# Second layer of a decoder kernel: GpSimd adds the exponentials of all six key tiles before TensorE sums them

## What is computed

```python
q = (Q @ Wq + bq).reshape(B, L, H, E)
k = (K @ Wk + bk).reshape(B, S, H, E)
v = (V @ Wv + bv).reshape(B, S, H, E)
scores = jnp.einsum('blhe,bshe->bhls', q, k)
A = jax.nn.softmax(scale * scores, axis=-1)
out = jnp.einsum('bhls,bshd->blhd', A, v).reshape(B, L, H * E)
return out @ We + be
```

## Time and profile before

| | |
|---|---|
| runs | 4483.24, 4483.69, 4485.51 us |
| the profiled execution | 4486.9 us |
| its span in the trace | 4485.1 us |
| mean granted TensorE clock | 0.864 |
| layer 2 in the trace | about 1380 to 2995 us |
| TensorE busy | 3463.7 us (77%) |
| VectorE, ScalarE, GpSimd busy | 57%, 38%, 14% |

### The profile page before, as it was taken

How to read it: one execution, slowest core, us unless ns; L and a number is a source line. 1 busy time by engine, 2 the same in 40 slices (tenths; PEclk the granted TensorE clock), 3 DMA queues, 4 the chain that set the end, 5 groups by cost and what they waited for, 6 DMA issues and landing times. The chain is left out here.

```text
span 4485.1 us, 77233 instructions
## 1 busy us (share of the span) xinstructions
PE 3463.7 (77%) x31129; PEld 2505.9 (56%) x31170; DVE 2556.4 (57%) x3681; ACT 1686.0 (38%) x3064; POOL 607.0 (14%) x371
## 2 busy tenths in 40 slices
PE   0887731149564999999999999959982399999990
PEld 0333311136324777777777777735552399899880
DVE  8679878879872455554555555537764133333325
ACT  2222379978321333333333333312220133333322
POOL 0000000000000222223222223220102300000005
PEclk9998865555686999999999999969996699999995
DMA  3400132323032011100011000022101422222217
GB/s 145 164 1 1 35 93 77 92 71 101 23 122 93 20 32 46 31 28 28 28 32 49 29 28 28 10 56 43 39 29 46 165 88 79 79 93 79 79 43 261
DMA packets 143861, 289.63 MB, mean 65 GB/s; under 512 B 43960, under 2 KB 43960, under 8 KB 139472
## 3 DMA queue, kind: packets, MB, share of 16 engines
q1 hardware_dynamic: 134608, 258.69, 18.4%
q0 software_dynamic: 8960, 26.58, 1.7%
HBM read 172.42 MB, written 100.93 MB: 61 GB/s over the span
## 5 line engine op out<-in xcount | busy, mean ns | idle before, releaser
L1568 DVE TENSOR_REDUCE arena<-psum 112x4 f32<-112x1504 f32 x256 | 440.3, 1720 | 323.2 <-PE psum L1389 322.7
L1303 POOL TENSOR_TENSOR arena<-arena 125x896 f32<-125x896 f32 x192 | 404.2, 2105 | 1139.5 <-ACT arena L1533 1139.5
L1533 ACT ACTIVATE arena<-psum 125x1792 f32<-125x1792 f32 x192 | 320.2, 1668 | 313.4 <-PE psum L1403 313.4
L779 ACT ACTIVATE arena<-arena,scales 112x224 bf16<-112x224 int8 x512 | 286.0, 559 | 36.1 <-DVEq L764 36.0
L694 PE MATMUL psum<-arena 64*112 64x224 bf16 x512 | 63.7, 401 | 276.2 <-DVEq L763 261.7
L2431 DVE TENSOR_TENSOR gelu_T_rest<-arena,gelu_T_high 128x384 fp32r<-128x384 f32 (+1 forms) x192 | 104.6, 547 | 269.5 <-ACT gelu_T_high L2394 269.5
L2309 PE MATMUL psum<-tokens_T_high,w_high 128*128 128x384 f32 (+1 forms) x768 | 255.2, 332 | 1.7 <-DVE tokens_T_rest L2423 1.6
L2311 PE MATMUL psum<-tokens_T_high,w_rest 128*128 128x384 f32 (+1 forms) x768 | 254.4, 331 | 0.0
L2310 PE MATMUL psum<-tokens_T_rest,w_high 128*128 128x384 f32 (+1 forms) x768 | 254.2, 331 | 0.0
L1558 DVE SCALAR_TENSOR_TENSOR k_T_rest<-psum,arena,k_T_high 128x376 fp32r<-128x376 f32 x128 | 77.9, 609 | 288.5 <-ACT k_T_high L1514 288.5
L1310 PE MATMUL psum<-Wv_high,ctx_T_high 128*125 128x256 f32 x768 | 231.4, 301 | 0.0
(11 more groups left out here) (352 smaller groups left out, 8645.0 us busy)
## 6 DMA issues: line engine op xcount, KB each, us to landing
arena<-L_ffn_moe_w SPq DMA_DIRECT2D x16, 2048.0 KB, 11.0
arena<-ctx SPq DMA_DIRECT2D x16, 1500.0 KB
rows_by_slot<-arena SPq DMA_DIRECT2D x1, 17920.0 KB, 51.0
arena<-x SPq DMA_DIRECT2D x14, 1024.0 KB, 13.5
arena<-arena SPq DMA_DIRECT2D x16, 896.0 KB
arena<-x_after_attn SPq DMA_DIRECT2D x32, 448.0 KB, 15.1
dots_ints<-arena SPq DMA_DIRECT2D x16, 784.0 KB, 4.8
arena<-dots_ints SPq DMA_DIRECT2D x16, 784.0 KB, 5.8
```

Source lines behind the costliest of these rows:

```text
L779: last = S.activation(junk[:, hg % 2, j, :], d8[:, u, h, (j % 2) * NS:(j % 2 + 1) * NS], ACT.Exp, bias=col("lowest")[0:HALF], scale=col("m ...
L1303: G.tensor_tensor(pair2[:, t, :, :], prob[:, t, :, 0:NS], prob[:, t, :, NS:2 * NS], ALU.add).then_inc(paired, 1)
L1533: S.activation(prob[:, t, :, :], score_psum(MC, 2 * NS), ACT.Exp, scale=SCALE2).then_inc(exp_done, 1)
L1568: return V.tensor_reduce(rmx[:, i // 2, i % 2, :], score_psum(HALF, HC), axis=AX.X, op=ALU.max).then_inc(r_free, 1)
```

## The change

A buffer `all_exps` of two halves (one for even groups, one for odd) takes the place of `pair2`. GpSimd now runs one addition after the first exponential of a group (tile 0 plus tile 1) and two after each of the others, each of which adds one more key tile of 125 x 896 onto `all_exps` in place: five additions a group for three, each but the first behind a wait for the one before. TensorE multiplies with ones once a group, for all six tiles. This one `sums` no longer stands after slot(0) but after `next_scores(0)`, slot(1) and `next_max(1)` of the next group. On VectorE `attend` moves with it, behind the second `reduce_max`. In `WINDOWS` the units `O` move from slots 3 and 5 of group 0 to slots 5 and 6, slot 2 of group 0 is left empty, and units of `C` and `VV` move back by up to three slots.

```diff
-        pair2 = sb("exps_of_key_pairs", [MC, TP, GH, NS], F32, L2)
+        all_exps = sb("exps_added_over_key_tiles", [MC, 2, GH, NS], F32, L2)
+        ADDS = 2 * TP - 1
...
-            (((Q, 3),), ((K, 6),), ((K, 7),), ((O, 0),), ((C, 0), (C, 1)), ((O, 1),), ((C, 2), (C, 3))),
-            (((C, 4), (C, 5)), ((K, 0),), ((C, 6), (C, 7)), ((K, 1),), ((VV, 0),), ((VV, 1), (VV, 2)), ((Q, 0),)),
-            (((Q, 1),), ((K, 2),), ((VV, 3),), ((K, 3),), ((VV, 4),), ((VV, 5),), ((VV, 6),)),
+            (((Q, 3),), ((K, 6),), (), ((K, 7),), ((C, 0), (C, 1)), ((O, 0),), ((O, 1),)),
+            (((C, 2), (C, 3)), ((K, 0),), ((C, 4), (C, 5)), ((K, 1),), ((C, 6), (C, 7)), ((VV, 0), (VV, 1)), ((Q, 0),)),
+            (((Q, 1),), ((K, 2),), ((VV, 2),), ((K, 3),), ((VV, 3),), ((VV, 4), (VV, 5)), ((VV, 6),)),
...
+                                n = b * NG2 + g
+                                added = n * ADDS + ADDS + max(0, 2 * t - 1)
                                 pool.wait_ge(exp_done, i + 1)
-                                pool.wait_ge(sum_mm, i + 1)
-                                G.tensor_tensor(pair2[:, t, :, :], prob[:, t, :, 0:NS], prob[:, t, :, NS:2 * NS], ALU.add).then_inc(paired, 1)
+                                if t == 0:
+                                    pool.wait_ge(sum_mm, n + 1)
+                                    G.tensor_tensor(all_exps[:, g % 2, :, :], prob[:, t, :, 0:NS], prob[:, t, :, NS:2 * NS], ALU.add).then_inc(paired, 1)
+                                else:
+                                    for s in range(2):
+                                        pool.wait_ge(paired, added + s)
+                                        G.tensor_tensor(all_exps[:, g % 2, :, :], all_exps[:, g % 2, :, :], prob[:, t, :, s * NS:(s + 1) * NS],
+                                                        ALU.add).then_inc(paired, 1)
...
-                def sums(n, g, t):
-                    pe.wait_ge(paired, n * TP + (t + 1 + TP))
+                def sums(n, g):
+                    pe.wait_ge(paired, n * ADDS + 2 * ADDS)
...
-                            if t >= 1:
-                                sums(n, g, t - 1)
                         next_max(0)
                         dense((M, g), b, b_next, b_before, u, first, last)
                         slot(0)
-                        if not (first and g == 0):
-                            sums(n - 1, (g - 1) % NG2, TP - 1)
                         for t in range(TP):
                             next_scores(t)
                             slot(2 * t + 1)
                             next_max(t + 1)
+                            if t == 0 and not (first and g == 0):
+                                sums(n - 1, (g - 1) % NG2)
                             slot(2 * t + 2)
                             next_values(t)
...
                         slot(0)
-                        if not (first and g == 0):
-                            attend(n - 1, (g - 1) % NG2, ch)
                         for t in range(TP):
                             slot(2 * t + 1)
                             if more:
                                 reduce_max(n + 1, t + 1)
+                            if t == 0:
+                                if not (first and g == 0):
+                                    attend(n - 1, (g - 1) % NG2, ch)
                             slot(2 * t + 2)
```

More of the change, by code:

```diff
@@ L1413, in values @@
                     last.then_inc(av_mm, 1)
-                def sums(n, g, t):
-                    pe.wait_ge(paired, n * TP + (t + 1 + TP))
+                def sums(n, g):
+                    pe.wait_ge(paired, n * ADDS + 2 * ADDS)
                     for j in range(GH):
-                        last = PE.matmul(psum[DH2 * j:DH2 * (j + 1), 6 + g % 2, NS:2 * NS], ones[0:MC, 0:DH2], pair2[:, t, j, :],
-                                         start=False, stop=(t == TP - 1))
+                        last = PE.matmul(psum[DH2 * j:DH2 * (j + 1), 6 + g % 2, NS:2 * NS], ones[0:MC, 0:DH2], all_exps[:, g % 2, j, :],
+                                         start=False, stop=True)
                     last.then_inc(sum_mm, 1)
@@ L1489, in final @@
                 def final():
-                    sums(NB * NG2 - 1, NG2 - 1, TP - 1)
+                    sums(NB * NG2 - 1, NG2 - 1)
                     for i in range(2):
@@ L1531, in body @@
                             act.wait_ge(av_mm, n * TP + (t + 1))
-                            act.wait_ge(paired, n * TP + (t + 1))
+                            act.wait_ge(paired, n * ADDS + (2 * t + 1))
                             S.activation(prob[:, t, :, :], score_psum(MC, 2 * NS), ACT.Exp, scale=SCALE2).then_inc(exp_done, 1)
@@ L1577, in attend @@
                 def attend(n, g, ch):
-                    dve.wait_ge(sum_mm, n * TP + 2 * TP)
+                    dve.wait_ge(sum_mm, n + 3)
                     ch.link(V.reciprocal(inv[:, :], psum[:, 6 + g % 2, NS:2 * NS]))
@@ L1595, in body @@
                         slot(0)
-                        if not (first and g == 0):
-                            attend(n - 1, (g - 1) % NG2, ch)
-                        else:
-                            dve.sem_inc(dch, 1)
-                        ch.n, ch.base = 0, n * 3 + 3
                         for t in range(TP):
@@ L1604, in body @@
                                 reduce_max(n + 1, t + 1)
+                            if t == 0:
+                                if not (first and g == 0):
+                                    attend(n - 1, (g - 1) % NG2, ch)
+                                else:
+                                    dve.sem_inc(dch, 1)
+                                ch.n, ch.base = 0, n * 3 + 3
                             slot(2 * t + 2)
@@ L1610, in first @@
                     dve.sem_inc(av_mm, TP)
-                    dve.sem_inc(sum_mm, TP)
-                    dve.sem_inc(paired, TP)
+                    dve.sem_inc(sum_mm, 2)
+                    dve.sem_inc(paired, ADDS)
                     dve.sem_inc(attended, 2)
```

## The result

The changed kernel takes 4561.61 us (median of 4 runs, 4557.98 to 4566.79), the kernel before 4484.60 in the same comparison: a ratio of 1.0169, 95% interval 1.0153 to 1.0185. It is 77 us slower. The forecast was 4570, the range 4505 to 4602.

What follows compares the result with a forecast made beforehand. TensorE bounds layer 2 (busy 95.00 of 96 us). Fifteen batches at +3.2 us give +48, the last batch +6, the clock +33: +87 on the profiled 4486.9, 4574, or 4570 us against the median; range 4505 to 4602.

Steps and rivals of the forecast that it cites:

- `(K, 1)`: Group 1, steady batch: TensorE waits 2.1 us, since VectorE splits context tiles 4 and 5 only behind reduction, reciprocal and multiplication.
- Second score pair of group 0: With slot 2 empty, TensorE waits 0.9 us for the reduction of the maxima ahead of these scores.
- First maxima transpose: From group 3 to group 0: GpSimd's bias addition holds up `combine` on VectorE, so TensorE waits 2.0 us.
- Small waits: Per batch, 1.4 us before first score pairs that lose `sums` as cover, and 1.0 us for PSUM banks.
- Savings: Each batch drops eight `sums` from TensorE, each worth 0.39 us, saving 3.1 us a batch.
- Last batch and end: No dense units for a next batch and one more addition before the last product: +6 us, between 2 and 10.
- The clock, its sum: New TensorE idle stretches bring half clock for 3.3 us, losing 1.65 us each: 20 x 1.65 = +33 us.
- The clock, its places: Of 30 new idle stretches of 2.1 and 2.0 us, two of three drop the clock: 20.
- Rival 1: The waits come, but the clock does not fall: 4537 us, chance 0.17.
- Rival 2: GpSimd does not hold up `combine`; VectorE's three short instructions slip through between two additions: 4524 us, chance 0.13.
- Rival 3: Faster: in group 1 VectorE reaches the split of context tiles 4 and 5 in time: 4434 us, chance 0.06.
- Rival 5: Worse: at half clock maxima quarters come late and one low stretch brings the next: 4612 us, chance 0.08.

Runs made afterwards that it cites:

- the run with the short filling: The changed kernel with TensorE given 8 filler products ahead of group 0's maxima transpose and 4 ahead of `(K, 1)`: 4534.34 us (ratio 1.0105).

## Why the prediction was right, step by step

- *Bound and period.* Layer 2 is bound by TensorE, and a steady batch was to take 99 to 101 us: it takes 97.8 to 102.5, on average 100.5. Right.
- *`(K, 1)`*: forecast 2.1 us, measured 2.01 in the trace, and shown as a cause by the run with `attend` moved (50 us, with the half clock that went with it).
- *Second score pair of group 0*: forecast 0.9, measured 0.97. No run took it away alone.
- *First maxima transpose*: forecast 2.0, measured 1.93 to 2.03, and the cause shown by the run with the bias addition moved (45 us, with the half clock that went with it). The instruction of `combine` that was held is the second, where the forecast had the first or the third.
- *Small waits*: forecast 2.4 us a batch, too much. The trace has 0.54 and 0.23 before first score pairs and 0.15 before `(K, 0)`, 0.9 us in all. The bounds were right, the middle was not: reductions nearly fitted behind the dense units, and PSUM turns hardly waited.
- *Savings*: forecast 3.1 us a batch, 0.39 a product. Measured: 0.38 a product, 3.0 a batch. But where only the products are left out the batch is 2.4 us shorter, mostly since maxima transposes lose them as cover. The sum had this cover at the first score pairs alone.
- These two errors are of opposite sign. Without the clock a steady batch was to grow by 3.2 us and grows by 2.6 (98.4 against 95.8).
- *Last batch and end*: forecast +6, measured +6.9, in part by luck. The wait ahead of the last product was forecast to grow by 2.1 us and grew by 2.6. But leaving out products alone made the last batch 3.9 us longer, at a lower granted clock, and the sum has no clock for that batch. The last product before and after:

```profile
2982.70 0.97 PE L1418 MATMUL psum<-arena,ones 125*32 125x224 f32 x8 [0.82 <-POOL arena L1303]
3061.70 0.97 PE L1427 MATMUL psum<-arena,ones 125*32 125x224 f32 x8 [3.42 <-POOL arena L1311]
```

- *The clock, its sum*: forecast 20 stretches of 3.3 us at 1.65 us each, 33 us in all. Measured in the 14 steady batches: 20 stretches, two of them of double length, so 22 times 3.4 us. They cost 30 us there by the run with the short filling, 1.4 us each, and 27 us between the medians of the runs. With the bias addition moved a stretch costs 1.1 us (97.8 against 96.7). So the price was too high and the count too low, and the two nearly cancel. (The fallen stretch of rows 8 is 3.4 us long, not 3.3.)
- *The clock, its places*: that two of three waits drop the clock was taken from one of two stretches in the first batch. Here it was 22 of 29, so the count was right by luck: a wait of that length alone does not decide it. Half clock followed waits of 1.93 to 2.03 us in 15 of 15 places before `(K, 1)` and in 7 of 14 before the maxima transpose here, in 7 of 15 with the bias addition moved, in 7 of 14 with `attend` moved, in 6 of 14 with the additions alone, and in 3 of 14 steady batches with the transpose behind slot 0. What decides it stays open.
- *Rival 1* (no fallen clock) fell, since stretches of 2.0 us were enough. The Trainium skill, TensorE: Matmul & The Clock Gate, "Why this matters for your kernels", asks for a longer idle stretch before the clock falls. These traces do not agree with it.
- *Rival 2* (`combine` slips through) fell: it slips in with one instruction, 0.65 us long, and the next is caught for 2.29 to 2.39 us. *Rival 3* (faster) fell with the wait of 2.01 us; it would have needed all waits below 4.2 us a batch, and there are 5.9. *Rival 5* (low stretches that bring the next) showed in 2 of 14 steady batches, where the clock stayed low for 6.8 us around the transpose.
- *The range*: by the bounds that the prediction gives for it, its upper end is 4607 and not 4602 (20 us for small waits and end, 17 for the clock, on 4570). Nothing hangs on it.

## What to carry to other kernels

Before giving work of the bounding engine to an idle one, look at what is queued behind the longer work and at who else it holds up. Here GpSimd was busy 28 of 96 us and in time for its own product, but an instruction queued behind its additions held up `combine`, and VectorE's `attend`, moved to make place for them, came ahead of a split that TensorE needed. Make such a change alone first: the additions alone, without the moves meant to support them, were in time and 50 us faster than with them. An idle stretch of 2 us on TensorE can cost more than itself: here half clock followed it in 22 of 29 places, at 1.4 us for each 3.4 us of it. And prices of single moves need not add: two that each took 45 to 50 us off took 81 together, because the clock was counted in both.

## What the runs showed of the hardware that was not expected

VectorE's `tensor_scalar` from one SBUF tensor of 112 x 8 fp32 to a bf16 one is held up by a running GpSimd addition. I had left that open. By line in the kernel after (duration ns min/median/max):

```profile
L1581 DVE TENSOR_SCALAR arena<-arena x64: 183/186/2387, 1460.6 to 3041.2; 112x8 bf16<-112x8 f32 x64
```

Against 187 ns at most before it now takes 2.29 to 2.39 us in 14 batches, each time until the bias addition ends. The Trainium skill, SBUF — State Buffer, "Who interferes with whom", lists this operation among those that can take the shared ports, and these rows agree. It also says that the one which starts first keeps them. The rows at the end of a batch agree: the bias addition started at 2060.82, the `tensor_scalar` at 2060.84, and the `tensor_scalar` ended when the bias addition had ended, at 2063.2.
